# A state-space scan on one Trainium2 core: rows of C moved by 14 columns, seven more products with B on GpSimd, ScalarE's steps reordered in the first and last chunk

## The chip, the core and the metric

The program runs on one core of a Trainium2 chip. A core has five engines that run their own instruction streams and meet at semaphores: TensorE (PE in the profile, PEld for its weight loads), VectorE (DVE), ScalarE (ACT), GpSimd (POOL) and SyncE (SP), whose queue issues the DMAs here. The metric is the device time of the whole program in microseconds; lower is better.

## The reference

Four layers follow each other on an activation of 4 x 1024 x 256 numbers: a Mamba block, a feed-forward block with retrieved experts, a linear attention block, and the feed-forward block again. The change is in the Mamba block alone. After projections, a convolution of four taps and silu, it computes for each token `delta`, `Bm` and `Cm` and then a recurrence along the tokens with 512 channels and 16 states:

```
def step(h, inp):
    d_l, b_l, c_l, x_l = inp
    h = jnp.exp(d_l[:, :, None] * A) * h + (d_l * x_l)[:, :, None] * b_l[:, None, :]
    y_l = jnp.einsum('ben,bn->be', h, c_l)
    return (h, y_l)
```

Then `y + x * W_D`, a product with `silu(skip)`, an output projection, and the residual.

## The kernel before, in words

The tokens are handled in 8 chunks of 512 (`CHUNKS`, c below; an even chunk starts a sequence, an odd chunk continues it). The 512 channels lie as 4 blocks of 128 partitions, and a pass over a chunk takes 2 of them. A *unit* M is one of the 16 states in one pass: 32 units in a chunk, 256 in all; i is a unit's number in its chunk. A unit's work goes round the engines:

- ScalarE computes the decays, exp(delta * A), one per block, into one of three PSUM slots (`decay`, L796).
- (delta * x) times the row of B goes into one of six slots of the buffer U. VectorE does it (L950) from a row that TensorE has spread over the partitions in PSUM (`spread_B`, L524), or GpSimd does it (L363, three units ahead, `AHEAD`) from a row fetched by DMA into the buffer B. Which units are GpSimd's stands in `FIRST_POOL` (first 16 units) and `ON_POOL`.
- VectorE runs the recurrence over the 512 tokens, two scans in a unit (L967), in place in U, one column to the right of a slot's start.
- GpSimd multiplies the scanned state by the row of C (L396), writing it one column to the left, at the slot's start. Rows of C are fetched by DMA into a ring of eight rows of 512 columns, buffer C. The last unit's product is VectorE's.
- TensorE adds up the states with eight transposing matmuls (`nsum`, L543).

Around this, each chunk's projections are computed a chunk ahead, a step in each unit. The tables `PE_AT`, `ACT_AT`, `DVE_AT` and `POOL_AT` say which step an engine does in unit i, after that unit's own work; an engine does all its work in that order, so a step that waits holds up what stands behind it. `"first"` replaces slots in the first chunk, `"late"` adds steps in the last. The steps named below: `in` and `cv` (input projection and convolution of a block, copied out of PSUM by ScalarE: L695, L704), `silu_x` (silu of the convolved chunk, L775) and `silu_g` (silu of the gate, L787), each with a table load ahead and behind, `double` (L650, four instructions on the residual), `sum` and `square` (L731, L738: row statistics of a later chunk), and `gate` (VectorE, L935). In unit M ScalarE first does the two decays of unit M + 1, and only then its steps.

Semaphores bind the rings: decay number s waits until scan s - 3 is done; a product with B for unit M waits until unit M - 6 is summed (`nsum_done`); SyncE's queue issues the fetches in order, each behind the GpSimd product that frees its slot.

The built program puts U at byte 181,216 of a partition, C at 205,856 and B at 222,240.

Of the kernel before, what the change touches and what calls it, by code (L numbers as in the profile page):

```python
# [14 lines left out]
P = 128  # L15
BATCH, SEQ, D = 4, 1024, 256
TOKENS = BATCH * SEQ
CHUNK = 512
CHUNKS = TOKENS // CHUNK
TILES = CHUNK // P  # L20
KD = D // P
E, N, R, TAPS = 512, 16, 128, 4
# [5 lines left out]
def need(eng, sem, value):  # L28

    if isinstance(value, int) and value <= 0:  # L30
        return
    eng.wait_ge(sem, value)
# [28 lines left out]
PASSES = 2  # L61
PE_E = KE // PASSES
UNITS = PASSES * N
ALL_UNITS = CHUNKS * UNITS


def mamba(nc, res, dram, shared, norms):
# [7 lines left out]

    WARM = 4
    U_RING, C_RING, A_RING, B_RING = 6, 8, 3, 2
    FIRST_POOL, AHEAD = (3, 7, 10, 12, 15), 3
    ON_POOL = ((2, 4, 7, 9, 12, 14), (3, 7, 11, 14), (2, 4, 6, 9, 11, 13, 15), (2, 5, 8, 11, 14))
    ctx = ExitStack()  # L80
    with ctx:
        def sb(name, shape, dt=FP32):
            return ctx.enter_context(nc.sbuf_tensor("m_" + name, shape, dt))
# [39 lines left out]
        def blocks(quarter):  # L123
# [7 lines left out]
        stack = sb("stack", [P, 2, CHUNK], FP32R)  # L131
        U = sb("U", [P, U_RING, PE_E, CHUNK + 1])
        state, weighted = U[:, :, :, 1:], U[:, :, :, 0:CHUNK]
        C = sb("C", [P, C_RING, CHUNK])
        B = sb("B", [P, B_RING, CHUNK + 1])[:, :, 1:]
        rows = sb("rows", [2 * N, CHUNK])
        bc_rows = nc.dram_tensor("bc_rows", (2, 2 * N, CHUNK), FP32, kind="Internal").ap()
# [43 lines left out]
                          for d, name in ((0, "turn0"), (0, "turn1"), (2, "query"))] + [(29, "back1", CHUNKS - 1)]}  # L181
# [6 lines left out]
                  "late": [(0, "sum", 8), (1, "square", 8), (2, "sum", 9), (3, "square", 9), (7, "norm", 8),  # L188
                           (8, "sum", 10), (9, "turn0", 8), (9, "turn1", 8), (10, "norm", 9), (11, "query", 8),
                           (12, "turn0", 9), (12, "turn1", 9), (14, "query", 9), (16, "square", 10), (18, "sum", 11),  # L190
                           (19, "square", 11), (20, "norm", 10), (21, "high0", 0), (22, "turn0", 10),
# [61 lines left out]
            c, q, p, n = place(M)  # L253
            return UNITS // 2 * (c // 2) + (N * p + n) // 2 + 1

        pool_units = [M for M in range(ALL_UNITS) if M % N in (ON_POOL[M // N % (2 * PASSES)] if M >= N else FIRST_POOL)]
        BEFORE = [len([m for m in pool_units if m < M]) for M in range(ALL_UNITS)]

        def pair(p):
# [8 lines left out]
        def _(sp):  # L268
# [20 lines left out]
            for M in range(ALL_UNITS):  # L289
# [21 lines left out]
                if FETCH <= M < FETCH + PARTS:  # L311
                    i, at = (M - FETCH) // KE, slice(CHUNK * ((M - FETCH) % KE), CHUNK * ((M - FETCH) % KE + 1))
                    sp.dma_start(shared.even[:, i, at], dram["ffn_w"][:, i, at]).then_inc(w_ffn, 16)
                need(sp, hc_ready, M - C_RING + 1)
                sp.dma_start(C[:, M % C_RING, :],
                             bc_rows[q, N + n:N + n + 1, :].to_broadcast([P, CHUNK])).then_inc(C_ready[M % C_RING], 16)
# [311 lines left out]
        def _(act):  # L628
# [153 lines left out]
            def silu_gate(k):  # L782

                for t in range(TILES):
                    wait_freed(act, f"sk{t}", k)
                g = gate[k % 2][:, :, :]
                nc.scalar.activation(g, g, ACT.Silu).then_inc(gate_ready, 1)  # L787
# [47 lines left out]
            for M in range(ALL_UNITS):  # L835
                if M == 0:
                    part("dl2", 0)
                ahead = M + 2 if M < 2 else M + 1
                if M != 2 and ahead < ALL_UNITS:
                    decay(PE_E * ahead)  # L840
                    decay(PE_E * ahead + 1)
                if M == 0:
                    part("sk3", 0)
                elif M == 1:
                    part("dt3", 0)
                elif M == 3:
                    part("dl3", 0)
                elif M in (5, 8):
                    part("double", M // 8)
                for name, k in parts_of(ACT_AT, M):  # L850
                    if name[:4] == "silu" and (name, k) != ("silu_g", 0):
                        (silu_x if name == "silu_x" else silu_gate)(k)
                        if (name, k) == ("silu_x", 1):
                            silu_gate(0)
                        nc.scalar.preload_act_table_set(EXP_LN_SET)
                    elif name[:4] == "silu":
                        continue
                    else:
                        part(name, k)
            for name in ("high2", "high3"):  # L860
# [1454 lines left out]
```

## Time and profile before

| | us |
|---|---|
| median of 3 runs (lowest, highest) | 1789.19 (1787.57, 1790.89) |
| the profiled execution | 1791.06 |
| its span, first to last instruction | 1789.3 |
| of which the 8 chunks of scans (31.6 to 851.6) | 820.0 |

The span is what the rows below divide up; 1.8 us of the execution lie outside it. Instructions of one engine overlap a little at their ends: for work back to back, the distance between two starts is what an instruction costs, and it is some hundredths of a us less than the duration shown (four in 8.60 us with the next start at 8.57, for one). "Idle before" an instruction names what ended the wait.

### The profile page before, as it was taken

Reading aid. Unit: us, or ns where it says so; the run is one execution under the profiler, and the core shown is the slowest. Engines: PE = TensorE matmul, PEld = TensorE weight load, DVE = VectorE, ACT = ScalarE, POOL = GpSimd, SP = SyncE. Lnnn points to the kernel's source line nnn. Section 1 sums busy time; section 2 is a strip of 40 time slices with the busy share of each in tenths; the row PEclk is TensorE's granted clock in tenths of the full one; section 3 lists DMA queues with packets and bytes.
Section 4 is the critical chain, followed back from the end, with each engine's and each line's share of the span. In section 5 each row is a group of like instructions: output and inputs, shape, how many; then the busy total and the mean of one; then the engine's idle time right before and its main releaser. Section 6 shows DMA issues by size and latency. Waiting matters only on the chain. (4 is left out here: it accounts for less than half of the span.)

```text
span 1789.3 us, 26479 instructions
## 1 busy us (share of the span) xinstructions
PE 1686.4 (94%) x9294; PEld 1330.9 (74%) x9294; DVE 1453.3 (81%) x2301; ACT 1068.6 (60%) x1872; POOL 1063.4 (59%) x668
## 2 busy tenths in 40 slices
PE   8989999899999999877999999999999999999999
PEld 3556666666766666566888888888899788888888
DVE  6899999999999999999877777775366876666665
ACT  7887887878887886878443444433444444344442
POOL 3899999999999998999722222221445322222220
PEclk9999999999999999989999999999999999999999
DMA  6323433343433334362011111121000021111111
GB/s 214 107 94 111 120 112 114 105 127 107 115 106 111 122 109 119 97 214 80 17 38 26 29 33 36 34 54 30 1 0 1 1 60 44 45 43 48 48 47 38
DMA packets 116542, 132.18 MB, mean 74 GB/s; under 512 B 19008, under 2 KB 65216, under 8 KB 116288
## 3 DMA queue, kind: packets, MB, share of 16 engines
q1 hardware_dynamic: 116416, 130.59, 25.4%
q8 instruction: 69, 1.13, 0.2%
q14 instruction: 57, 0.47, 0.1%
HBM read 102.22 MB, written 4.72 MB: 60 GB/s over the span
## 5 line engine op out<-in xcount | busy, mean ns | idle before, releaser
L396 POOL TENSOR_TENSOR m_U<-m_U,m_C 128x1024 f32<-128x1024 f32 x255 | 554.3, 2193 | 43.0 <-DVE m_U L967 43.0
L543 PEld LDWEIGHTS m_y<-ident,m_U 128*128 128x128 f32 x2048 | 248.5, 146 | 106.7 <-issue 72.6
L967 DVE TENSOR_TENSOR_SCAN m_U<-m_dA,m_carry,m_U 128x512 f32<-128x512 f32 x256 | 309.8, 1264 | 9.3 <-ACT m_dA L796 8.5
L967 DVE TENSOR_TENSOR_SCAN m_U<-m_dA,m_U 128x512 f32<-128x512 f32 x256 | 295.2, 1204 | 11.3 <-ACT m_dA L796 11.3
L543 PE MATMUL m_y<-ident,m_U 128*128 128x128 f32 x2048 | 280.0, 282 | 20.0 <-POOL m_U L396 19.5
L796 ACT ACTIVATE m_dA<-high,m_negA 128x512 f32<-128x512 f32 x256 | 170.9, 684 | 57.1 <-DVE m_U L967 56.6
L796 ACT ACTIVATE m_dA<-even,m_negA 128x512 f32<-128x512 f32 x256 | 169.5, 683 | 42.0 <-DVE m_U L967 40.2
L1266 POOL TENSOR_TENSOR SW<-g_Rt 128x512 f32<-128x512 f32 x32 | 39.7, 1271 | 256.8 <-DMA g_CT<-SW 237.1
L1266 POOL TENSOR_TENSOR SW<-f_Rt 128x512 f32<-128x512 f32 x32 | 41.0, 1309 | 213.4 <-DMA f_CT<-SW 213.4
L524 PE MATMUL m_psB<-m_stack,m_pick 128*128 128x512 f32 x169 | 86.1, 509 | 40.0 <-DVE m_U L950 38.1
L1455 ACT ACTIVATE g_sil<-g_psG 128x512 f32<-128x512 f32 x64 | 38.3, 599 | 126.9 <-PE g_psG L1325 126.9
L1455 ACT ACTIVATE f_sil<-f_psG 128x512 f32<-128x512 f32 x64 | 38.3, 598 | 126.3 <-PE f_psG L1325 126.2
L1368 PE MATMUL f_psO<-weights_hi,f_H_hi 128*128 128x256 f32 x384 | 108.9, 284 | 4.8 <-DVE f_H_lo L1622 4.7
L1368 PE MATMUL g_psO<-weights_hi,g_H_hi 128*128 128x256 f32 x384 | 108.4, 282 | 0.7 <-DVE g_H_lo L1622 0.6
L1368 PE MATMUL f_psO<-weights_hi,f_H_lo 128*128 128x256 f32 x384 | 107.5, 280 | 0.0
L1368 PE MATMUL f_psO<-weights_lo,f_H_hi 128*128 128x256 f32 x384 | 107.5, 280 | 0.0
L1368 PE MATMUL g_psO<-weights_hi,g_H_lo 128*128 128x256 f32 x384 | 107.2, 279 | 0.0
L1368 PE MATMUL g_psO<-weights_lo,g_H_hi 128*128 128x256 f32 x384 | 107.2, 279 | 0.0
L433 PE MATMUL m_job<-turned 128*128 128x512 f32 x224 | 106.1, 596 | 0.7 <-ACT even L713 0.5
L950 DVE TENSOR_TENSOR m_U<-even,m_psB 128x1024 f32<-128x1024 f32 x88 | 105.1, 1195 | 0.6 <-PE m_psB L524 0.6
L1618 DVE TENSOR_TENSOR zns<-g_psU,g_sil 128x512 f32<-128x512 f32 x64 | 44.0, 688 | 73.9 <-PE g_psU L1325 72.5
L1842 POOL TENSOR_TENSOR a_rinv<-a_ssq,a_mhalf 128x64 f32<-128x64 f32 x6 | 63.2, 10549 | 59.0 <-DVE a_ssq L2117 59.0
(412 smaller groups left out, 4459.3 us busy)
## 6 DMA issues: line engine op xcount, KB each, us to landing
m_C<-bc_rows SPq DMA_DIRECT2D x256, 256.0 KB, 3.2
m_B<-bc_rows SPq DMA_DIRECT2D x87, 256.0 KB, 3.5
f_CT<-SW SPq DMA_DIRECT2D x128, 64.0 KB, 2.1
g_CT<-SW SPq DMA_DIRECT2D x128, 64.0 KB, 2.1
even<-in_ffn_w SPq DMA_DIRECT2D x16, 256.0 KB, 5.4
g_z_raw<-g_turned_z SPq DMA_DIRECT2D x112, 32.0 KB, 1.9
out<-res SPq DMA_DIRECT2D x7, 512.0 KB, 2.8
res<-in_x SPq DMA_DIRECT2D x1, 3072.0 KB, 12.6
```

The source lines that it names most:

```text
L396: pool.tensor_tensor(weighted[:, at, :, :], state[:, at, :, :], C[:, M % C_RING, :].unsqueeze(1).to_broadcast([P, PE_E, CHUNK]), ALU.mult) ...
L433: ins = nc.tensor.matmul(out, w, x, start=first and k == 0, stop=last and k == len(pairs) - 1)
L524: nc.tensor.matmul(psB[:, :], pick[:, n:n + 1].to_broadcast([P, P]), stack[:, q, :], start=True, stop=True).then_inc(B_full, 1)
L543: last = nc.tensor.matmul(y[:, t, j * P:(j + 1) * P], weighted[:, M % U_RING, j, t * P:(t + 1) * P], ident[:, :], start=False, stop=n == N ...
L796: nc.scalar.activation(dA[:, s % A_RING, :], delta[q][:, e, :], ACT.Exp, scale=negA[:, e, n:n + 1]).then_inc(dA_ready, 1)
L950: nc.vector.tensor_tensor(state[:, M % U_RING, :, :], dx[q][:, pair(p), :], psB[:, :].unsqueeze(1).to_broadcast([P, PE_E, CHUNK]), ALU.mul ...
L967: nc.vector.tensor_tensor_scan(u, dA[:, s % A_RING, :], u, carry[:, e, n:n + 1] if q else 0.0, ALU.mult, ALU.add).then_inc(scan_done, 1)
L1266: pool.tensor_tensor(S[:, j, :, :], Rt[:, j // 2, 0, j % 2, 0:TOP].unsqueeze(2).to_broadcast(SPREAD), Rt[:, j // 2, 1, j % 2, :].unsqueeze ...
L1368: last = nc.tensor.matmul(psO[:, j // 2, (j % 2) * D:(j % 2 + 1) * D], H[a][:, i % RING, j * P:(j + 1) * P], lower[b][:, i, :], start=i == ...
L1455: nc.scalar.activation(to[:, i % 2, :], psG[:, i % 2, :], ACT.Silu).then_inc(g_free, 1)
L1618: nc.vector.tensor_tensor(to, u, s, ALU.mult).then_inc(u_free, 1)
L1842: pool.tensor_tensor(rinv[:, at, :], ssq[:, at, :], mhalf[:, :, :], ALU.pow).then_inc(rinv_ready, 1)
```

## The change

C's buffer gets 14 more columns, and its rows begin 14 columns (56 bytes) further; U stays, B and what lies behind it moves by 64 bytes (B to 222,304). GpSimd's units are now given for all 16 passes: 9 in chunk 0 as before (three of them others), 13 instead of 12 in chunks 1, 3, 5 and 7, 11 instead of 10 in chunks 2, 4 and 6; 94 in all instead of 87. In the first chunk ScalarE does `double` in units 6 and 17 and no longer in 5 and 8, `cv0` and `in1` in unit 5 and no longer in 4, and the gate's silu for chunk 0 in unit 15, by itself, and no longer right behind `silu_x` in unit 13. In the last chunk `sum` and `square` for piece 9 move from units 2 and 3 to units 3 and 6.

```diff
-    FIRST_POOL, AHEAD = (3, 7, 10, 12, 15), 3
-    ON_POOL = ((2, 4, 7, 9, 12, 14), (3, 7, 11, 14), (2, 4, 6, 9, 11, 13, 15), (2, 5, 8, 11, 14))
+    EVEN, ODD, AHEAD = ((1, 3, 5, 7, 9, 11, 13), (3, 7, 11, 14)), ((1, 3, 5, 7, 9, 11, 13), (2, 4, 7, 9, 12, 14)), 3
+    ON_POOL = ((3, 7, 9, 11, 13), (3, 7, 11, 14)) + (ODD + EVEN) * (CHUNKS // 2 - 1) + ((1, 4, 7, 9, 12, 14), (2, 4, 6, 8, 10, 12, 14))
...
-        C = sb("C", [P, C_RING, CHUNK])
+        C = sb("C", [P, C_RING * CHUNK + 14])[:, 14:].rearrange("p (r t) -> p r t", r=C_RING)
...
-                  "first": {3: (), 4: ("cv0", "in1")},
-                  "late": [(0, "sum", 8), (1, "square", 8), (2, "sum", 9), (3, "square", 9), (7, "norm", 8),
+                  "first": {2: (), 3: (), 4: (), 5: ("cv0", "in1"), 15: ("silu_g",)},
+                  "late": [(0, "sum", 8), (1, "square", 8), (3, "sum", 9), (6, "square", 9), (7, "norm", 8),
...
-                elif M in (5, 8):
-                    part("double", M // 8)
+                elif M in (6, 17):
+                    part("double", M // 17)
                 for name, k in parts_of(ACT_AT, M):
-                    if name[:4] == "silu" and (name, k) != ("silu_g", 0):
+                    if name[:4] == "silu":
                         (silu_x if name == "silu_x" else silu_gate)(k)
-                        if (name, k) == ("silu_x", 1):
-                            silu_gate(0)
                         nc.scalar.preload_act_table_set(EXP_LN_SET)
-                    elif name[:4] == "silu":
-                        continue
```

On ScalarE, in the first chunk around units 3 to 9 (m_dA: decays, high: `cv`, turned: `in`, res: `double`, m_rn: `sum`):

```order
 L796 ACTIVATE m_dA<-even,m_negA 128x512 x2
 L713 ACTIVATE even<-m_job 128x512
-L796 ACTIVATE m_dA<-even,m_negA 128x512 x2
+L796 ACTIVATE m_dA<-even,m_negA 128x512 x4
 L704 ACTIVATE high<-m_job,m_convb 128x512
 L695 ACTIVATE turned<-m_job 128x512
 L796 ACTIVATE m_dA<-even,m_negA 128x512 x2
 L650 ACTIVATE res<-res,m_sc 128x256 x4
-L796 ACTIVATE m_dA<-even,m_negA 128x512 x2
-L704 ACTIVATE high<-m_job,m_convb 128x512
-L796 ACTIVATE m_dA<-even,m_negA 128x512 x2
-L695 ACTIVATE turned<-m_job 128x512
```

Two more decays stand ahead of the first convolution's copy. On the same engine in units 13 to 17 (L775: `silu_x`, L787: `silu_g`), now:

```order
81 L775 ACT_TABLE_LOAD
82 L775 ACTIVATE high<-high 128x2048
83 L853 ACT_TABLE_LOAD
84 L796 ACTIVATE m_dA<-even,m_negA 128x512 x4
85 L787 ACT_TABLE_LOAD
86 L787 ACTIVATE even<-even 128x2048
87 L853 ACT_TABLE_LOAD
```

Before, L787 stood directly behind L775 with one table load on each side of the pair; now four decays stand between the two, and there are two table loads more. On VectorE in the middle of chunk 1 (the rows with m_psB are its products with B), before:

```order
95 L967 SCALAR_TENSOR_TENSOR m_U<-m_dA,m_carry,m_U 128x512 x4
96 L950 TENSOR_TENSOR m_U<-high,m_psB 128x2x512
97 L967 SCALAR_TENSOR_TENSOR m_U<-m_dA,m_carry,m_U 128x512 x4
98 L950 TENSOR_TENSOR m_U<-high,m_psB 128x2x512
99 L967 SCALAR_TENSOR_TENSOR m_U<-m_dA,m_carry,m_U 128x512 x2
```

and now, where the same instructions have the lines 963 and 946:

```order
94 L963 SCALAR_TENSOR_TENSOR m_U<-m_dA,m_carry,m_U 128x512 x4
95 L946 TENSOR_TENSOR m_U<-high,m_psB 128x2x512
96 L963 SCALAR_TENSOR_TENSOR m_U<-m_dA,m_carry,m_U 128x512 x2
97 L946 TENSOR_TENSOR m_U<-high,m_psB 128x2x512
98 L963 SCALAR_TENSOR_TENSOR m_U<-m_dA,m_carry,m_U 128x512 x2
99 L946 TENSOR_TENSOR m_U<-high,m_psB 128x2x512
100 L963 SCALAR_TENSOR_TENSOR m_U<-m_dA,m_carry,m_U 128x512 x2
```

Both pieces run from the scans of units 11 and 12 to those of unit 15. Between them VectorE made two products (for units 14 and 16) and makes three now (14, 15 and 16); the product for unit 1 has gone to GpSimd instead, and of units 2 to 13 VectorE makes six before and now.

## Rows read from the trace of the kernel before

**Rows 1.** The page, part 1: busy time, share and instructions by engine.
```profile
PE 1686.4 (94%) x9294; PEld 1330.9 (74%) x9294; DVE 1453.3 (81%) x2301; ACT 1068.6 (60%) x1872; POOL 1063.4 (59%) x668
```

**Rows 2.** Windows by chunk (0, 1, 2, 7, rest): length, busy time by engine, clock, DMA.
```profile
31.60:143.30 111.70, 95.42 (x426) 58.46 (x424) 102.21 (x93) 90.59 (x159) 95.72 (x66) 0.96 0.34 112
...
143.30:245.50 102.20, 96.24 (x471) 65.53 (x469) 100.36 (x87) 82.25 (x140) 100.30 (x56) 0.97 0.39 115
245.50:345.20 99.70, 93.70 (x471) 63.62 (x471) 98.66 (x89) 82.07 (x140) 96.97 (x66) 0.99 0.37 111
...
749.20:851.60 102.40, 74.17 (x418) 60.46 (x418) 98.36 (x85) 83.69 (x174) 99.48 (x63) 0.87 0.43 137
851.60:1789.30 937.70, 919.58 (x5570) 812.07 (x5570) 637.21 (x1558) 386.50 (x686) 269.56 (x162) 1.00 0.14 32
```

**Rows 3.** Waits in chunks 1 to 6: total us, times, longest.
```profile
DVE m_U L967 <- ACT m_dA L796: 8.5, 12, 1.4
...
POOL m_U L396 <- DVE m_U L967: 14.7, 19, 1.2
...
PE m_psB L524 <- DVE m_U L950: 16.3, 26, 1.4
```

**Rows 4.** Groups of instructions by form, up to 860 us: busy us, mean ns.
```profile
L396 POOL TENSOR_TENSOR m_U<-m_U,m_C 128x1024 f32<-128x1024 f32 x255 | 554.3, 2193 | 43.0 <-DVE m_U L967 43.0
...
L363 POOL TENSOR_TENSOR m_U<-high,m_B 128x1024 f32<-128x1024 f32 x48 | 96.4, 2008 | 0.0
...
L352 POOL TENSOR_TENSOR high<-high 128x512 f32<-128x512 f32 x16 | 20.7, 1291 | 0.0
...
L381 POOL TENSOR_TENSOR turned<-ident,m_convw 128x512 f32<-128x512 f32 x4 | 4.0, 1038 | 0.0
...
L345 POOL TENSOR_TENSOR m_sc<-m_sc,m_off 128x8 f32<-128x8 f32 x7 | 1.4, 203 | 0.1
```

**Rows 5.** Timeline of GpSimd around the end of chunk 1: start, length, instruction.
```profile
238.95 8.60 POOL L396 TENSOR_TENSOR m_U<-m_U,m_C 128x1024 f32<-128x1024 f32 x4
247.52 1.99 POOL L363 TENSOR_TENSOR m_U<-even,m_B 128x1024 f32<-128x1024 f32 x1
249.47 4.32 POOL L396 TENSOR_TENSOR m_U<-m_U,m_C 128x1024 f32<-128x1024 f32 x2
```

**Rows 6.** Timeline of VectorE in chunks 1 and 2, units 13 to 16.
```profile
183.47 4.79 DVE L967 TENSOR_TENSOR_SCAN m_U<-m_dA,m_carry,m_U 128x512 f32<-128x512 f32 x4
188.19 1.19 DVE L950 TENSOR_TENSOR m_U<-high,m_psB 128x1024 f32<-128x1024 f32 x1
190.80 2.46 DVE L967 TENSOR_TENSOR_SCAN m_U<-m_dA,m_carry,m_U 128x512 f32<-128x512 f32 x2 [1.42 <-ACT m_dA L796]
...
291.48 2.34 DVE L967 TENSOR_TENSOR_SCAN m_U<-m_dA,m_U 128x512 f32<-128x512 f32 x2 [0.57 <-ACT m_dA L796]
```

**Rows 7.** Timeline of VectorE in chunk 0: the scans behind a wait.
```profile
57.16 2.34 DVE L967 TENSOR_TENSOR_SCAN m_U<-m_dA,m_U 128x512 f32<-128x512 f32 x2 [3.52 <-ACT m_dA L796]
...
70.42 4.57 DVE L967 TENSOR_TENSOR_SCAN m_U<-m_dA,m_U 128x512 f32<-128x512 f32 x4 [0.86 <-ACT m_dA L796]
...
88.44 2.34 DVE L967 TENSOR_TENSOR_SCAN m_U<-m_dA,m_U 128x512 f32<-128x512 f32 x2 [3.40 <-ACT m_dA L796]
```

**Rows 8.** Timeline of ScalarE in chunk 0.
```profile
54.16 0.69 ACT L704 ACTIVATE high<-m_job,m_convb 128x512 f32<-128x512 f32 x1 [3.54 <-PE m_job L433]
...
57.60 2.06 ACT L650 ACTIVATE res<-res,m_sc 128x256 f32<-128x256 f32 x4
...
61.29 0.69 ACT L704 ACTIVATE high<-m_job,m_convb 128x512 f32<-128x512 f32 x1 [0.44 <-PE m_job L433]
...
84.44 1.89 ACT L787 ACTIVATE even<-even 128x2048 f32<-128x2048 f32 x1
86.35 1.28 ACT L855 ACT_TABLE_LOAD   x1
```

**Rows 9.** Timeline of VectorE in chunk 7, units 4 and 5.
```profile
764.59 2.46 DVE L967 TENSOR_TENSOR_SCAN m_U<-m_dA,m_carry,m_U 128x512 f32<-128x512 f32 x2 [2.54 <-ACT m_dA L796]
767.78 2.46 DVE L967 TENSOR_TENSOR_SCAN m_U<-m_dA,m_carry,m_U 128x512 f32<-128x512 f32 x2 [0.73 <-ACT m_dA L796]
```

**Rows 10.** The page, part 6: DMA issues, KB each, us to landing.
```profile
m_C<-bc_rows SPq DMA_DIRECT2D x256, 256.0 KB, 3.2
m_B<-bc_rows SPq DMA_DIRECT2D x87, 256.0 KB, 3.5
```

More of the change, by code:

```diff
@@ L254, in copied @@
             return UNITS // 2 * (c // 2) + (N * p + n) // 2 + 1
-        pool_units = [M for M in range(ALL_UNITS) if M % N in (ON_POOL[M // N % (2 * PASSES)] if M >= N else FIRST_POOL)]
+        pool_units = [M for M in range(ALL_UNITS) if M % N in ON_POOL[M // N]]
         BEFORE = [len([m for m in pool_units if m < M]) for M in range(ALL_UNITS)]
```

## The prediction

> **What bounds the kernel now.** I read the windows by chunk first. Of 1789.3 us, 937.7 lie behind the scans, where nothing changes [rows 2]; the change lives in the 820 us of the eight chunks. There three engines are nearly full, which the page's shares over the whole span hide [rows 1]. In chunk 1 VectorE works 100.4 us of 102.2, GpSimd 100.3 and TensorE 96.2; in chunk 2 it is 98.7, 97.0 and 93.7 of 99.7 [rows 2]. The waits come second: in the six middle chunks VectorE waits 8.5 us in all, always for a decay from ScalarE, GpSimd 14.7 us for scans, and TensorE 16.3 us for VectorE's products [rows 3]. VectorE is thus the engine that sets the pace; GpSimd is as full in the odd chunks and has 1.7 us more room in the even ones; and every long wait of VectorE's is ScalarE's doing. The timelines come last and place those waits: in chunk 0 before units 6, 10 and 15, 3.52 + 0.86 + 3.40 us [rows 7], in chunk 7 before units 4 and 5, 2.54 + 0.73 us [rows 9], and in the middle chunks 1.42 us before unit 15 of an odd and 0.57 us of an even one [rows 6].
>
> **The seven products.** One more unit in each of chunks 1 to 7 goes from VectorE to GpSimd. VectorE loses 7 products: 1.19 us each, less the 0.07 by which neighbours overlap (four scans of 4.79 us in all have the next start at 4.72), so 1.11 us, 7.8 us in all [rows 6]. GpSimd gains 7 at 249.47 - 247.52 = 1.95 us [rows 5], 13.7 us more, in the scans' shadow only if it has room. It has 102.2 - 100.3 = 1.9 us in an odd chunk and 2.7 in an even one [rows 2]. So without anything else GpSimd would be full in the odd chunks. TensorE spreads seven rows fewer, which nobody waits for.
>
> **The rows of C.** This decides whether that room exists. No row shows a product with C at the new place, so I bound it. GpSimd's two-input products differ in time for the same size: 512 columns take 1.291 us where both inputs and the output start at the same place modulo 2048 bytes (`dx`, L352), and 1.038 us for L381, whose inputs start over 1,000 bytes apart modulo 2048 but also repeat elements [rows 4]. With the 0.203 us of an eight-column product taken as fixed, 1024 columns would take 2 x 1.291 - 0.2 = 2.38 us in the one case and 2 x 1.038 - 0.2 = 1.88 us in the other. Between these lie the two measured at 1024: 2.193 for C and 2.008 for B [rows 4]. From the buffers' places, C's rows start 16 to 60 bytes beyond the state that they multiply (modulo 2048), B's rows 932 bytes or more from their other input. 14 columns make C's distance 72 to 116 bytes. I take B's 2.01 us, the nearest product of the same size whose inputs are not close, and keep 1.88 and 2.38 as ends. 32 products a chunk at 0.185 us less free 5.9 us: GpSimd then needs 100.3 + 1.95 - 5.9 = 96.4 us in an odd and 93.0 in an even chunk, below VectorE's 98 to 99. The gain over the present time is then VectorE's alone, since faster products with C take nothing off its path. GpSimd stops being the bound once 32 products save 2.1 us, at 2.13 us for one.
>
> The Trainium skill speaks against this: GPSIMD Engine Reference, Performance versus the Vector engine, gives about 2.6 cycles an element to any two-input product, from its two inputs sharing a read port, and knows no influence of where they lie. As an estimate from that page, 1024 elements would take 2.2 us before and after. C's 2.19 us agrees; B's 2.01 does not, nor does L352's 1.29 us where the rule gives 1.1. By the rule the sum would be that of the first rival below.
>
> The fetch of C's rows to the new place I cost at nothing: rows of B, which already start off by 4 bytes, land in 3.5 us against 3.2 [rows 10], and a ring of eight rows fetches 7 units, over 20 us, ahead.
>
> **Where the freed VectorE time goes: middle chunks.** In an odd chunk VectorE now has three products ahead of units 14, 15 and 16 instead of two, while ScalarE does `silu_x`. That covers 1.1 of the 1.42 us of wait before unit 15; I take 0.9, as in the even chunks a wait of 0.57 is left with this very pattern [rows 6]. Odd: 1.1 + 0.9 = 2.0 us, three chunks 6.0. Even: the product alone and 0.1 us of wait, 1.2, three chunks 3.6.
>
> **Chunk 0.** The wait of 3.52 us before unit 6 stands because ScalarE sits 3.54 us in the copy of `cv0` until TensorE has done the convolution [rows 7, 8], with the decays for unit 6 queued behind. Now the decays for units 5 and 6 go first, so unit 6 starts on time. But TensorE is late with the next piece as well: `cv1` arrives at 61.3 us whatever ScalarE does [rows 8], and the decays for unit 8 stand behind it, so they end at about 62.5. VectorE comes to unit 8 at about 59.4 and waits 3 us there, where the scan of unit 8 began at 63.9 before. Only 1.4 us are gained by then, of which 1.1 are a product with B that unit 9 gives to GpSimd earlier than unit 10 did. `double` out of unit 8 (2.0 us) removes the 0.86 before unit 10, and `silu_g` out of unit 13 (1.89 us) with one product more on VectorE takes the 3.40 down to some 0.4; the block moved to unit 15, 4.5 us with its own two table loads, costs 0.3 to 0.6 again, like its kind in even chunks. VectorE's share of products in the chunk is the same. Followed unit by unit, unit 17 then starts about 4 us earlier, and `double` in unit 17 and the gate at unit 18 stand in slots with room. I take 4.0; the ends are 1.5 (TensorE holds the pace of units 3 to 12) and 6.5.
>
> **Chunk 7.** `sum` out of unit 2 leaves only `silu_g` there: 1.8 to 2.0 us of the 2.54 go. The 0.73 before unit 5 goes too, since the product for unit 6 is VectorE's now. GpSimd's next use of these statistics is in unit 7, after the product with C, and `square` in unit 6 ends before. With the product moved: 2.7 + 1.1, of which I take 3.5, as ScalarE has `square` and `norm` next to each other now.
>
> **Sum.** 4.0 + 6.0 + 3.6 + 3.5 = 17.1 us. The lead of the decays before units 5 to 12 is only 1 to 2 us, and TensorE has 5 % left; I give back 1.6 for waits that this brings. So 1791.06 - 15.5 = 1775.6 for an execution like the profiled one; the median lies 1.9 us lower, hence 1773.7.
>
> **Rivals.**
> First, *the product with C keeps its 2.19 us*, since its price comes from writing one column beside its own input. For: the six slots of U put C 16 to 60 bytes away, and the products agree within 0.01 us, so distance may count for nothing. Then GpSimd is full in chunks 1 to 6: +0.5 us in odd ones, 0 in even ones; chunk 0 keeps its 4 us, chunk 7 gives 2: 1789.2 - 4.5 = 1784.7.
> Second, *ScalarE and TensorE take the gain*: C becomes cheaper, but the waits for decays come back elsewhere at half of what was removed. For: VectorE already meets decays with no lead at units 4 and 15; against: three of the four moves take work off ScalarE where it is late. 1789.2 - 8 = 1781.
> Third, and slower: *the new place is worse*, up to the 2.38 us bound. Place: L396 in all chunks; price 256 times the difference, since GpSimd is then the bound. From the first rival's 4.5 us of gain, the kernel turns slower by over 3.6 us from 8.1 / 256 = 0.03 us on, at 2.225 us; at 2.38 it is +48 - 4.5, 1833. Against it: 72 bytes is farther from the coincident case than 16.
> That the products don't move, or that the steps wait for something behind them, I exclude from the order of the instructions.
>
> **How the numbers follow.** What measurement tells from no change is 0.2 %, 3.6 us. Forecast 0.60 (1768 to 1780); first rival 0.20 (1781 to 1789, two thirds of it faster by over 3.6 us); second 0.10, faster; third 0.10, slower. Faster 0.60 + 0.10 + 0.13 = 0.83, same 0.07, slower 0.10. The range goes from 1766, where nearly all of VectorE's waits are gone in chunk 0, to 1788: it takes in the forecast and both mild rivals.
>
> **What the profile after would show.** L396 at 2.01 us or, by the rivals, at 2.19 or over 2.22: this one row decides most. L363 near 2.01, 94 of them, VectorE's products 161 in place of 168. Waits of VectorE in chunks 1 to 6 below 7 us, all for decays; 1.42 before unit 15 of an odd chunk down to about 0.5; GpSimd's waits for scans up from 14.7 to over 35 us. Chunk 0 at about 107.7, odd chunks 100.2, even ones 98.5, chunk 7 at 98.9. In chunk 0 the wait before unit 6 moves to unit 8. I am wrong if GpSimd waits less than now, if chunk 0 keeps its length, or if anything behind 852 us changes its length by over 1 us.

## The result and the profile after

| | before | after |
|---|---|---|
| median, us (lowest, highest, 10 runs each, same chip) | 1790.77 (1787.57, 1792.31) | 1795.76 (1793.62, 1796.91) |
| span of the profiled execution | 1789.3 | 1794.5 |

The ratio is 1.003, with a 95% interval of 1.0021 to 1.0039: the change makes the kernel 0.3% slower. The forecast was 1773.7, in a range that ended at 1788, with a chance of 0.10 for slower.

The row that was to decide most is that of the product with C. Groups of instructions by form in the profile after (busy us, mean ns of one, then the idle time ahead of them), to be set beside [rows 4]:

```profile
L396 POOL TENSOR_TENSOR m_U<-m_U,m_C 128x1024 f32<-128x1024 f32 x255 | 554.7, 2191 | 34.6 <-DVE m_U L963 34.6
L963 DVE TENSOR_TENSOR_SCAN m_U<-m_dA,m_carry,m_U 128x512 f32<-128x512 f32 x256 | 310.4, 1269 | 13.4 <-POOL m_U L363 8.7 <-ACT m_dA L796 4.0
L963 DVE TENSOR_TENSOR_SCAN m_U<-m_dA,m_U 128x512 f32<-128x512 f32 x256 | 295.9, 1207 | 15.0 <-POOL m_U L363 8.4 <-ACT m_dA L796 6.4
L363 POOL TENSOR_TENSOR m_U<-high,m_B 128x1024 f32<-128x1024 f32 x52 | 104.5, 2010 | 1.2 <-issue 1.2
L363 POOL TENSOR_TENSOR m_U<-even,m_B 128x1024 f32<-128x1024 f32 x42 | 84.2, 2004 | 0.5 <-PE m_y L543 0.5
L352 POOL TENSOR_TENSOR high<-high 128x512 f32<-128x512 f32 x16 | 20.5, 1282 | 0.0
```

It is 2191 ns, against 2193 before: the new place did nothing. GpSimd has the seven more products with B (94 in all) and no time saved for them. VectorE's scans waited almost only for decays before (0.6 us for L363):

```profile
L967 DVE TENSOR_TENSOR_SCAN m_U<-m_dA,m_carry,m_U 128x512 f32<-128x512 f32 x256 | 309.8, 1264 | 9.3 <-ACT m_dA L796 8.5 <-POOL m_U L363 0.6
L967 DVE TENSOR_TENSOR_SCAN m_U<-m_dA,m_U 128x512 f32<-128x512 f32 x256 | 295.2, 1204 | 11.3 <-ACT m_dA L796 11.3
```

Now they wait 17.1 us for L363 (8.7 + 8.4). Windows by chunk (0, 1, 2, 7, rest: length, then busy time by engine, clock, DMA), to be set beside [rows 2]:

```profile
32.10:138.60 106.50, 92.25 (x421) 56.65 (x420) 101.22 (x92) 92.10 (x160) 94.62 (x66) 0.98 0.36 116
138.60:241.70 103.10, 96.11 (x469) 63.65 (x468) 99.82 (x87) 82.59 (x140) 101.44 (x56) 0.98 0.38 116
241.70:343.50 101.80, 95.09 (x474) 63.88 (x473) 98.06 (x88) 82.39 (x141) 99.62 (x68) 0.99 0.40 112
753.00:856.60 103.60, 76.17 (x411) 63.48 (x410) 98.64 (x85) 84.53 (x175) 101.03 (x64) 0.81 0.45 139
856.60:1794.50 937.90, 921.08 (x5584) 813.29 (x5583) 638.59 (x1558) 386.69 (x686) 271.65 (x163) 1.00 0.14 32
```

Chunk 0 is 5.2 us shorter, chunks 1 to 6 are 8.5 us longer together (0.8 to 1.1 in an odd one, 1.6 to 2.1 in an even one), chunk 7 is 1.2 longer. The windows are cut at a chunk's first scan, and VectorE's product for a chunk's unit 1 stands just ahead of that scan (before: 1.19 us at 142.15, the scan at 143.26). Unit 1 is GpSimd's now in chunks 1 to 7, which takes this product out of the window of the chunk before: about 1.1 of chunk 0's 5.2 us belong to the table of chunk 1, as the run with that table alone shows below. What follows the scans has its length. VectorE's busy time in chunk 2 fell by 0.6 us while the chunk grew by 2.1, and GpSimd is busy for 99.6 of 101.8 and 101.4 of 103.1. The waits in chunks 1 to 6 (total us, times, longest), to be set beside [rows 3]:

```profile
DVE m_U L963 <- POOL m_U L363: 14.6, 24, 1.6
POOL m_U L396 <- DVE m_U L963: 12.3, 12, 1.3
PE m_psB L524 <- DVE m_U L946: 11.9, 29, 0.8
DVE m_U L963 <- ACT m_dA L796: 4.6, 12, 0.5
```

VectorE's waits for decays fell from 8.5 to 4.6, as forecast (below 7), but 14.6 us for GpSimd came in their place. GpSimd's own waits for scans fell from 14.7 to 12.3 us, which the prediction had named as a sign of being wrong. Where VectorE's waits stand is seen in the timelines of chunk 2, first pass (start, length, instruction, in brackets the idle time before it). GpSimd, then VectorE:

```profile
262.29 2.00 POOL L363 TENSOR_TENSOR m_U<-even,m_B 128x1024 f32<-128x1024 f32 x1
264.25 2.19 POOL L396 TENSOR_TENSOR m_U<-m_U,m_C 128x1024 f32<-128x1024 f32 x1
266.38 0.19 POOL L400 COPY m_carry<-m_U 128x4 f32<-128x4 f32 x1
266.52 2.18 POOL L396 TENSOR_TENSOR m_U<-m_U,m_C 128x1024 f32<-128x1024 f32 x1
268.66 2.00 POOL L363 TENSOR_TENSOR m_U<-even,m_B 128x1024 f32<-128x1024 f32 x1
```
```profile
264.32 4.57 DVE L963 TENSOR_TENSOR_SCAN m_U<-m_dA,m_U 128x512 f32<-128x512 f32 x4 [0.45 <-POOL m_U L363]
268.81 1.20 DVE L946 TENSOR_TENSOR m_U<-even,m_psB 128x1024 f32<-128x1024 f32 x1
270.69 4.57 DVE L963 TENSOR_TENSOR_SCAN m_U<-m_dA,m_U 128x512 f32<-128x512 f32 x4 [0.69 <-POOL m_U L363]
```

With a product with B every other unit, GpSimd needs 268.66 - 262.29 = 6.37 us for two units and VectorE, without its wait, 270.69 - 264.32 - 0.69 = 5.68. GpSimd loses its lead, and then each pair of units costs 0.69 us more. The waits come back at every other unit up to 13, 2.8 us in an even chunk. In an odd chunk they are 1.9 to 2.7 us, and most of it, 1.56 us, stands at unit 30, in the second pass.

In chunk 0 the wait of 3.52 us before unit 6 is gone; waits of 1.12 us before the product between the scans of units 6 and 7 and of 2.21 us before unit 8 stand in its place, and 3.40 us before unit 15 [rows 7] are 0.65:

```profile
57.40 1.22 DVE L946 TENSOR_TENSOR m_U<-even,m_psB 128x1024 f32<-128x1024 f32 x1 [1.12 <-PE m_psB L524]
63.09 2.34 DVE L963 TENSOR_TENSOR_SCAN m_U<-m_dA,m_U 128x512 f32<-128x512 f32 x2 [2.21 <-ACT m_dA L796]
85.28 2.34 DVE L963 TENSOR_TENSOR_SCAN m_U<-m_dA,m_U 128x512 f32<-128x512 f32 x2 [0.65 <-ACT m_dA L796]
```

The wait of 1.42 us before unit 15 of an odd chunk [rows 6] is down as well, here in chunk 1:

```profile
187.08 2.46 DVE L963 TENSOR_TENSOR_SCAN m_U<-m_dA,m_carry,m_U 128x512 f32<-128x512 f32 x2 [0.30 <-ACT m_dA L796]
```

In chunk 7, 2.54 and 0.73 us [rows 9] are 0.29 and nothing, and others appear further on:

```profile
767.48 2.46 DVE L963 TENSOR_TENSOR_SCAN m_U<-m_dA,m_carry,m_U 128x512 f32<-128x512 f32 x2 [0.29 <-ACT m_dA L796]
783.55 2.46 DVE L963 TENSOR_TENSOR_SCAN m_U<-m_dA,m_carry,m_U 128x512 f32<-128x512 f32 x2 [0.84 <-POOL m_U L363]
793.79 4.81 DVE L963 TENSOR_TENSOR_SCAN m_U<-m_dA,m_carry,m_U 128x512 f32<-128x512 f32 x4 [0.84 <-POOL m_U L363]
835.79 2.46 DVE L963 TENSOR_TENSOR_SCAN m_U<-m_dA,m_carry,m_U 128x512 f32<-128x512 f32 x2 [1.88 <-ACT m_dA L796]
```

### The profile page after: what moved, and what is told of

The parts are those of the page before. It is cut to its first block and busy times, and to the rows that moved or that the text cites. A ratio compares the mean times of both kernels' runs of the same rounds, so it can differ in the third digit from the quotient of the medians.

```text
span 1794.5 us, 26477 instructions
## 1 busy us (share of the span) xinstructions
PE 1691.0 (94%) x9287; PEld 1331.0 (74%) x9287; DVE 1450.0 (81%) x2294; ACT 1073.0 (60%) x1874; POOL 1076.9 (60%) x675
## 5 line engine op out<-in xcount | busy, mean ns | idle before, releaser
L396 POOL TENSOR_TENSOR m_U<-m_U,m_C 128x1024 f32<-128x1024 f32 x255 | 554.7, 2191 | 34.6 <-DVE m_U L963 34.6
L543 PE MATMUL m_y<-ident,m_U 128*128 128x128 f32 x2048 | 284.3, 285 | 35.6 <-POOL m_U L396 34.9
L363 POOL TENSOR_TENSOR m_U<-high,m_B 128x1024 f32<-128x1024 f32 x52 | 104.5, 2010 | 1.2 <-issue 1.2
L946 DVE TENSOR_TENSOR m_U<-even,m_psB 128x1024 f32<-128x1024 f32 x85 | 101.8, 1198 | 1.7 <-PE m_psB L524 1.7
```

The lines of the kernel that those rows point to most:

```text
L363: pool.tensor_tensor(state[:, M % U_RING, :, :], dx[q][:, pair(p), :], B[:, i % B_RING, :].unsqueeze(1).to_broadcast([P, PE_E, CHUNK]), AL ...
L396: pool.tensor_tensor(weighted[:, at, :, :], state[:, at, :, :], C[:, M % C_RING, :].unsqueeze(1).to_broadcast([P, PE_E, CHUNK]), ALU.mult) ...
L543: last = nc.tensor.matmul(y[:, t, j * P:(j + 1) * P], weighted[:, M % U_RING, j, t * P:(t + 1) * P], ident[:, :], start=False, stop=n == N ...
L946: nc.vector.tensor_tensor(state[:, M % U_RING, :, :], dx[q][:, pair(p), :], psB[:, :].unsqueeze(1).to_broadcast([P, PE_E, CHUNK]), ALU.mul ...
```

## Experiments: the change taken apart

Two questions stood after the traces: is the loss all in the middle chunks' table, and why is the product with C where it was? The next four kernels are each a part of the change, put on the kernel before.

**Only the rows of C moved.**

```diff
-        C = sb("C", [P, C_RING, CHUNK])
+        C = sb("C", [P, C_RING * CHUNK + 14])[:, 14:].rearrange("p (r t) -> p r t", r=C_RING)
```

> The kernel before with C's rows 14 columns further and nothing else. My theory: the place of C does nothing, the product with C (L396) stays at 2.19 us and the time within 2 us of before. The forecast's theory, which the trace after already speaks against: L396 at 2.01 us. A third: the move costs (B and the buffers behind C shift by 64 bytes, the rows' DMAs land unaligned), then L363 or the fetches get slower and the time rises by 2 us or more.

Measured: 1.0007 (0.9998 to 1.0016), no difference. Its row:

```profile
L396 POOL TENSOR_TENSOR m_U<-m_U,m_C 128x1024 f32<-128x1024 f32 x255 | 553.6, 2190 | 43.1 <-DVE m_U L967 43.1
```

The place of C alone changes neither price nor time, and the fetches land in 3.3 us against 3.2 [rows 10]. In the changed kernel they take 3.7 us, but so they do in the next run, where C is at its old place: that comes with the table and not with the address, and no wait of GpSimd's for them appears.

**Only the table of chunks 1 to 6.**

```diff
-    ON_POOL = ((2, 4, 7, 9, 12, 14), (3, 7, 11, 14), (2, 4, 6, 9, 11, 13, 15), (2, 5, 8, 11, 14))
+    EVEN, ODD = ((1, 3, 5, 7, 9, 11, 13), (3, 7, 11, 14)), ((1, 3, 5, 7, 9, 11, 13), (2, 4, 7, 9, 12, 14))
```

> The kernel before with the new list of GpSimd's units in chunks 1 to 6 alone (13 and 11 products a chunk). My theory: in passes with units 1, 3, ..., 13 on GpSimd two products with C and one with B take 6.2 us for each two units against VectorE's 5.6 to 5.8, VectorE waits for GpSimd's products, and chunks 1 to 6 get 8 to 9 us longer in all; the time is 7 to 10 us above before. The first rival's pricing: GpSimd is just full, chunks 1 to 6 change by +1.5 us at most. If the loss in the changed kernel came from ScalarE's or C's part, this one is near before or faster.

Measured: 1.0049 (1.0035 to 1.0062), 8 to 9 us slower, with VectorE's waits in chunks 1 to 6:

```profile
DVE m_U L967 <- POOL m_U L363: 14.8, 26, 1.6
DVE m_U L967 <- ACT m_dA L796: 5.2, 13, 0.7
```

The 14.8 us are those of the changed kernel (14.6). The loss is this table's, at a product of 2.19 us. Chunk 0, in which this run changes nothing, is 110.5 us against 111.7: the product for unit 1 of chunk 1 has left its end, and VectorE is busy there for 101.07 us against 102.21 [rows 2].

```profile
31.40:141.90 110.50, 94.19 (x421) 57.44 (x420) 101.07 (x92) 89.90 (x158) 94.64 (x66) 0.96 0.36 112
```

**Only ScalarE's order.** The ScalarE lines of the diff ("first", "late", `double`, `silu_g`), nothing else.

> The kernel before with ScalarE's new order in chunks 0 and 7 alone, all products where they were. My theory: chunk 0 is 3.5 to 5 us shorter (the wait before unit 6 gone, one of about 2.2 us at unit 8 in its place), chunk 7 1.5 to 2.5 us shorter, chunks 1 to 6 as before: 5 to 7.5 us faster. Rival: the gains belong to the products that moved with it (unit 9 in place of 10 in chunk 0, unit 6's in chunk 7) and ScalarE's order alone brings less than 3 us.

Measured: 0.9978 (0.9969 to 0.9987), 4 us faster, 1 us short of the low end expected. Chunk 0 is 108.0 us (111.7 before), chunk 7 100.8 (102.4), 3.7 and 1.6 us less and both at the low end of what was expected. The profiled executions differ by 6.1 us and the medians by 3.7; where the rest goes isn't shown, but what lies behind the chunks took 935.0 to 939.1 us in the profiles here, though no kernel changes it. The wait expected at unit 8 isn't there: VectorE waits 1.11 and 1.95 us for rows from TensorE, before two of its products.

**ScalarE's order and the new lists of chunks 0 and 7.**

```diff
+    FIRST, LAST = ((3, 7, 9, 11, 13), (3, 7, 11, 14)), ((1, 4, 7, 9, 12, 14), (2, 4, 6, 8, 10, 12, 14))
```

> ScalarE's new order and the new lists for chunks 0 and 7, but the old lists in chunks 1 to 6 and C at its old place. My theory: chunk 0 is 4 to 5 us shorter, chunk 7 0 to 1 us longer as in the changed kernel (13 products in it make GpSimd late at units 9, 12 and 25), so 3 to 5 us faster than before and 1 to 3 us slower than the kernel with ScalarE's order alone. Rival: chunk 7's loss in the changed kernel is inherited from the full GpSimd of chunks 1 to 6; then this one is the faster of the two, by 2 to 4 us.

Measured: 0.998 (0.9971 to 0.9989), as far below before as ScalarE's order alone; the 1 to 3 us between the two that were expected didn't show. Chunk 0 is 107.6 us, 4.1 shorter, and chunk 7 102.7: its 13 products give back the 1.6 us that ScalarE's order brings there, with a wait of 0.84 us for L363 at unit 12 and one of 1.85 for a decay at unit 25, though chunks 1 to 6 are the old ones. So most of that loss is chunk 7's own and not inherited; the wait at unit 9 isn't there and came with the middle chunks' table. Chunk 6 is 99.0 us against 99.7, since the product for unit 1 of chunk 7 has left its end, so that the 13th product costs about 1 us over both chunks. The three parts' ratios add to 1.0007 + 1.0049 + 0.998 - 2 = 1.0036, where the whole has 1.003: within the intervals nothing is left for an interplay.

## Experiments: what the product with C costs, and why

**Prices.** A kernel that leaves the order of work alone and varies what the product reads and writes; the four forms stand at lines 398, 400, 402 and 404. In odd chunks the second to fourth leave sums other than the reference's.

```diff
-        C = sb("C", [P, C_RING, CHUNK])
+        C = sb("C", [P, C_RING, CHUNK + 65])[:, :, 0:CHUNK]
...
-    U_RING, C_RING, A_RING, B_RING = 6, 8, 3, 2
+    U_RING, C_RING, A_RING, B_RING = 6, 7, 3, 2
...
+                    if q == 0 or M % 4 == 0 or M >= SECOND_LAST:
+                        pool.tensor_tensor(weighted[:, at, :, :], state[:, at, :, :], row, ALU.mult)
+                    elif M % 4 == 1:
+                        pool.tensor_tensor(state[:, at, :, :], state[:, at, :, :], row, ALU.mult)
+                    elif M % 4 == 2:
+                        pool.tensor_tensor(weighted[:, at, :, :], dx[q][:, pair(p), :], row, ALU.mult)
+                    else:
+                        pool.tensor_tensor(weighted[:, at, :, :], weighted[:, at, :, :], row, ALU.mult)
```

> The price of the product with C by itself, in the kernel before. C's ring has seven rows, each 260 bytes (an odd number of columns) further from the next modulo 2048 bytes, so that a row of C starts 20 to 1,060 bytes from the state it multiplies. In odd chunks the product has four forms by unit: as before (state to one column left), in place at the state's column, from dx instead of the state to the slot's start, and in place at the slot's start; the third and fourth leave y wrong in odd chunks. My theory: distance does nothing (2.19 us at all seven rows) and the 0.18 us above the product with B come from reading what is written one column beside: the third form, which has the operands of a product with B, takes 2.01 us, the in-place ones 2.19 or 2.01. The forecast's theory: far rows take 2.01 us or less, near ones 2.19. A third: the port is shared with TensorE or VectorE, and all forms take what falls beside them, spread over 1.9 to 2.3 us.

Measured once: 1791.85 us (before 1791.62). The groups of this run look like the kernel before:

```profile
L398 POOL TENSOR_TENSOR m_U<-m_U,m_C 128x1024 f32<-128x1024 f32 x183 | 398.9, 2192 | 38.6 <-DVE m_U L973 38.3
L404 POOL TENSOR_TENSOR m_U<-m_U,m_C 128x1024 f32<-128x1024 f32 x24 | 52.4, 2183 | 3.3 <-DVE m_U L973 3.3
L400 POOL TENSOR_TENSOR m_U<-m_U,m_C 128x1024 f32<-128x1024 f32 x24 | 51.7, 2156 | 0.9 <-DVE m_U L973 0.8
L402 POOL TENSOR_TENSOR m_U<-high,m_C 128x1024 f32<-128x1024 f32 x24 | 51.7, 2154 | 0.2
```

But these means hide three prices. The timeline of GpSimd in chunk 2 has neighbours that differ by 0.2 us at one line:

```profile
260.61 2.42 POOL L398 TENSOR_TENSOR m_U<-m_U,m_C 128x1024 f32<-128x1024 f32 x1 [1.43 <-DVE m_U L973]
...
267.19 2.22 POOL L398 TENSOR_TENSOR m_U<-m_U,m_C 128x1024 f32<-128x1024 f32 x1
...
271.29 2.04 POOL L398 TENSOR_TENSOR m_U<-m_U,m_C 128x1024 f32<-128x1024 f32 x1
```

None of the theories holds as written. A far row is not faster than a near one, the operands' kind does nothing, and what falls beside a product does nothing. The distance in hundreds of bytes sorts nothing either: slot 0 of U, with the rows of C, gives 2.20, 2.40, 2.18, 2.00, 2.18, 2.38, 2.18 us in turn. Sorted by the address of the first input less that of the second, modulo 16 bytes, for each of the two blocks of 512 elements, all 255 products fall into place (worked out from each one's length and the buffers' addresses):

```
first less second input, modulo 16: block 1, block 2     units   mean us of the forms
0, 4  (also 0, 0 and 4, 4)                                 61     2.36 to 2.38
4, 8                                                       66     2.18 to 2.19
12, 0                                                      62     2.18 to 2.19
8, 12 (also 8, 8 and 12, 12)                               66     2.00
```

So half a product, 512 elements with half of what is fixed, costs 1.19 us where the difference is 0 or 4 and 1.00 where it is 8 or 12. The lengths in the four classes don't overlap: 2.34 to 2.42, twice 2.17 to 2.24, and 1.99 to 2.04 us. Neither address alone does it: at L398, with the first block of the state 4 beyond a multiple of 16, rows of C at 0, 4, 8 and 12 give 2.19, 2.38, 2.19 and 2.00 us, and with it at 12 they give 2.18, 2.01, 2.19 and 2.37. Where the output goes makes no difference (L398 and L400 agree class by class within 0.01 us). This also explains the rows of before: a slot of U is 4,104 bytes, 8 modulo 16, and a block in it 2,052, 4 modulo 16. The state is therefore 4 and 8 beyond C in even slots and 12 and 0 in odd ones: one half slow and one fast in each. A shift by 14 columns is 8 modulo 16 and exchanges the two cases. With such slots any shift of C averages 2.19 us. B lies 12 or 8 off in all 87 products: 2.01. And `dx` (L352) has difference 0: 1.28 us.

Two pages of the Trainium skill bear on this. SBUF — State Buffer, Specifications (TRN2), gives the memory lines of 16 bytes, and a penalty for each crossing into a new line; it says nothing of two inputs' offset. The period found here is the same 16 bytes; that the lines cause it isn't shown. GPSIMD Engine Reference, 3. Performance versus the Vector engine, gives any two-input product about 2.6 cycles an element at 1.2 GHz: as an estimate 2.2 us for 1024, about what the slow case has without the 0.2 us that is fixed (2.38 - 0.20 = 2.18); the fast case, 1.80, lies below what the page calls the floor.

**What the schedule would do at 2.02 us.** The changed kernel with the product over 936 of 1024 elements.

```diff
-                    pool.tensor_tensor(weighted[:, at, :, :], state[:, at, :, :],
+                    pool.tensor_tensor(weighted[:, at, :, 0:468], state[:, at, :, 0:468],
```

> The changed kernel with its product with C over 468 of 512 columns (936 elements in place of 1024), which leaves 44 columns of each unit unmultiplied: by (2.19 - 0.20) / 1024 for an element it should take 2.02 us, what the forecast took for the product at the new place. If the product's price is the step that failed and the rest of the forecast holds, the time is 1774 (1768 to 1780) and VectorE waits for GpSimd's products under 3 us. If the forecast's other terms were wrong too, chunks 1 to 6 stay over 100 us each and the time is 1782 or more.

Measured: 1776.23, 0.9919 (0.9906 to 0.9933). The price came out at 2.03 us, scans waited 2.0 us for L363 in all, and chunks 1 to 6 lasted 99.1 to 101.0 us. With the price, the time is within the forecast's 1768 to 1780; chunk 7, at 100.4 us where 98.9 was forecast, isn't put right by it.

**Slots of 4,112 bytes, C three columns further.** On the kernel before, then on the changed one (the padded kernel below).

```diff
-        U = sb("U", [P, U_RING, PE_E, CHUNK + 1])
+        U = sb("U", [P, U_RING, PE_E * (CHUNK + 1) + 2])[:, :, 0:PE_E * (CHUNK + 1)].rearrange("p u (e t) -> p u e t", e=PE_E)
...
+        C = sb("C", [P, C_RING * CHUNK + 3])[:, 3:].rearrange("p (r t) -> p r t", r=C_RING)
```

> The kernel before with two columns of padding in each slot of U (so that a slot is 4,112 bytes, a multiple of 16, instead of 4,104) and C's rows 3 columns further; nothing else. From the 255 products with C in the run on prices: a half of a product (512 elements) takes 1.19 us where the address of the first input less that of the second is 0 or 4 modulo 16 bytes, and 1.00 where it is 8 or 12. Here the state lies 8 bytes (first block) and 12 bytes (second) beyond C modulo 16 in every slot, so L396 takes 2.00 us in all 255, without a row at 2.19. Rival: the padding or some other place decides, and L396 stays at 2.19 or splits. Time: GpSimd gets 6 us more room a chunk, but VectorE's path is as it was, so 0 to 4 us faster than before.

> The changed kernel with the same padding of U and C's rows 3 columns further in place of 14. Theory: the product takes 2.00 us in all slots, VectorE's waits for GpSimd's products go from 17 us to under 3, and the time is within 3 us of the run with the product cut to 936 columns: 1773 to 1779. Rival: that run gained from the columns left out (TensorE or the memory less busy), and with all columns at 2.00 us the time stays above 1782.

On the kernel before: 0.9999 (0.999 to 1.0008). On the changed kernel: 1774.05 us, 0.9906 (0.9891 to 0.9921), 17 us faster than the kernel before beside it (1791.07) and the fastest of all kernels here. The rows, of the first and the second:

```profile
L396 POOL TENSOR_TENSOR m_U<-m_U,m_C 128x1024 f32<-128x1024 f32 x255 | 508.8, 2008 | 86.2 <-DVE m_U L967 85.6
```
```profile
L396 POOL TENSOR_TENSOR m_U<-m_U,m_C 128x1024 f32<-128x1024 f32 x255 | 510.9, 2018 | 56.8 <-DVE m_U L963 54.5 <-PE m_y L543 1.8
L963 DVE TENSOR_TENSOR_SCAN m_U<-m_dA,m_carry,m_U 128x512 f32<-128x512 f32 x256 | 309.7, 1262 | 3.9 <-ACT m_dA L796 2.7 <-POOL m_U L363 1.3
```

The price fell to 2.01 and 2.02 us, with no product above 2.08. With the old table the 45 us saved turned into waiting (43.0 to 86.2 us) and bought nothing; with the new table they carry the seven products. Windows of the second kernel's chunks 0, 1, 2 and 7:

```profile
31.90:138.70 106.80, 94.62 (x428) 58.78 (x427) 101.29 (x92) 92.16 (x160) 91.18 (x67) 0.95 0.36 116
138.70:238.40 99.70, 93.32 (x464) 62.32 (x463) 99.14 (x86) 82.45 (x140) 94.58 (x55) 0.99 0.43 120
238.40:337.30 98.90, 95.17 (x485) 65.54 (x484) 97.62 (x88) 82.11 (x140) 95.20 (x69) 0.99 0.37 116
...
735.40:836.40 101.00, 72.66 (x413) 58.65 (x412) 98.41 (x85) 84.43 (x175) 94.29 (x63) 0.86 0.45 141
```

**C one column further instead of three**, on the kernel before with the same slots: both blocks slow.

> The kernel before with the padding of U and C's rows 1 column further: first block 0, second block 4 bytes modulo 16 beyond C, in every slot. Two columns, 8 bytes, from the kernel with 3. Theory: L396 takes 2.37 us in all 255 units, GpSimd is the bound, and the time is 255 x 0.19 = 47 us above before, less the 15 us that GpSimd waits for scans in the middle chunks and some 10 in the outer ones: 1815 to 1835. Rival: with rows this near the state, nothing but the padding counts, and the price is as with 3 columns.

Measured once: 1817.19 us, 26 above before.

```profile
L396 POOL TENSOR_TENSOR m_U<-m_U,m_C 128x1024 f32<-128x1024 f32 x255 | 601.3, 2385 | 23.2 <-DVE m_U L967 23.2
```

Two columns of a buffer's place, with the same schedule, are 0.38 us a product and 27 us in all. The products took 47 us more of GpSimd (601.3 against 554.3), of which 20 came out of its waiting for scans (43.0 to 23.2).

## Experiments: how full GpSimd may be

**Ten products a chunk, but dense**, on the kernel before.

```diff
+    EVEN = ((1, 3, 5, 7, 9, 11, 13), (3, 7, 11))
```

> The kernel before with the even chunks' first pass on the new list (units 1, 3, ..., 13) and their second on 3, 7 and 11: ten products a chunk, as many as before. My theory: where GpSimd's products stand counts, not their sum; with one every other unit GpSimd falls behind by 0.3 to 0.6 us for each two units in the first pass, VectorE waits there for 1.5 to 3 us, and in the second pass VectorE has one product more and cannot catch up: 1.5 to 2.5 us a chunk, 5 to 8 us in all. The rival, that GpSimd's load over the whole chunk sets the time: within 1 us a chunk of before, 0 to 2 us in all.

Measured: 1.0035 (1.0022 to 1.0049). Even chunks last 103.2 us against 99.7, odd ones 0.5 to 1.4 less than before, as the product for an even chunk's unit 1 has left their end; both together are 2.6 longer. VectorE waited 6.2 us for L363 in chunks 1 to 6, and made one product more in the second pass, where GpSimd had time over. The same number of products in worse places costs 6 to 7 us. Chunk 2:

```profile
243.90:347.10 103.20, 94.01 (x472) 62.91 (x469) 100.12 (x90) 82.82 (x141) 99.55 (x68) 0.99 0.35 111
```

**Eleven, spread**, with ScalarE's new order and the new list of chunk 0.

```diff
+    EVEN = ((2, 4, 7, 9, 12, 14), (2, 5, 8, 11, 14))
```

> ScalarE's new order, the new list for chunk 0, the old ones for odd chunks and 7, and in even chunks eleven products, spread as 2, 4, 7, 9, 12, 14 and 2, 5, 8, 11, 14. As many products as the changed kernel has in even chunks, without its dense pass. My theory: even chunks get up to 1.1 us shorter than the 99.7 of before, since both passes have room on GpSimd: 1781 to 1785, up to 3 us faster than with the old lists. The rival by total load: GpSimd full at 99 us, even chunks as before or up to 1 us longer: 1786 to 1788.

Measured: 1784.81 us, 0.9965 (0.9952 to 0.9979). The time alone lies in the range of my theory, but ScalarE's order alone had 0.9978, and the intervals overlap, so it doesn't decide. The lengths do: even chunks took 99.6 to 100.8 us, no less than with ten, and GpSimd is busy for 98.5 of 100.3 in chunk 2. By them my theory of a gain was wrong and the rival by total load right.

```profile
240.70:341.00 100.30, 94.19 (x468) 63.97 (x469) 97.86 (x89) 82.07 (x140) 98.54 (x67) 0.99 0.37 112
```

Both counts matter: at 2.19 us eleven products fill GpSimd's even chunk, and set densely, as in the changed kernel, they cost another 1.5 us a chunk.

**One product more in each of chunks 1 to 6, at 2.01 us.**

```diff
+    EVEN, ODD = ((1, 3, 5, 7, 9, 11, 13), (2, 5, 8, 11, 14)), ((1, 3, 5, 7, 9, 11, 13), (2, 4, 6, 8, 10, 12, 14))
```

> The kernel of the run before this one with one more product with B on GpSimd in each of chunks 1 to 6: 14 in odd ones, 12 in even ones. GpSimd has about 5 us of room in an odd and 3.5 in an even chunk and needs 2.0 more; VectorE loses 1.1 us a chunk. If VectorE sets the pace there, up to 6 us faster than the run before; if TensorE (94 us of 99) or GpSimd's delays in a dense pass take over, no gain or 1 to 4 us slower.

Measured: 1777.19, 0.9928 (0.9915 to 0.9942), 3 us slower than the padded kernel. Even chunks are 0.4 us shorter (98.5), odd ones 1 to 2 us longer (101.5): scans wait 6.1 us for L363 again, most of it in the odd chunks' second dense pass. Twelve in even chunks with 13 in odd ones wasn't tried; as an estimate from these lengths it would bring about 1 us.

## Why the prediction was wrong, step by step

- **The rows of C: wrong, and the step that failed.** The prediction took B's 2.01 us for the new place, on a distance modulo 2048 bytes. It measured 2191 ns. With it went the 5.9 us of room a chunk that the sum rested on: the middle chunks, forecast 9.6 us shorter, are 8.5 longer. What counts is the offset modulo 16 bytes, and 56 bytes only exchange the two kinds of slots. The bounds, from L352 and from L381, held: the worst case was put at 2.38 us and measured 2.385; the best, 1.88, was reached nowhere, the fast kind takes 2.00. But between the bounds the value was chosen by likeness in size, where the rows already held a hint against it, which the first rival names: a product whose mean is within 0.01 us of 2.19 in all six slots shows no trace of a distance that varies from 16 to 60 bytes, and nothing showed why one of 72 to 116 should act.
- **The seven products: right.** GpSimd's busy time in chunks 1 and 2 rose by 1.1 and 2.7 us. VectorE makes 161 products in 193.0 us where it made 168 in 200.6. Its whole busy time fell by 3.3 us only (1453.3 [rows 1] to 1450.0): its scans take 1.3 us more in all and the work behind the chunks 1.4, and 1.6 us stay unplaced. In the padded kernel, where it waits little, it is busy for 1.2 us less in chunk 1 and 1.0 less in chunk 2, which is the 1.1 us a product of the forecast.
- **The fetches at nothing: right**, 3.3 us against 3.2 in the run with C alone, and nobody waits for the 3.7 of the changed kernel.
- **Middle chunks: right on its condition.** With the product at 2.02 us (padded slots) the odd chunks are 6.3 us shorter in all against 6.0 forecast, the even ones 2.8 against 3.6. The wait before unit 15 of an odd chunk fell from 1.42 [rows 6] to 0.30 us even in the changed kernel. GpSimd's waits for scans were forecast at over 35 us and are 28.1; the forecast's own lengths gave no more, 3 x (100.2 - 96.4) + 3 x (98.5 - 93.0) = 27.9.
- **Chunk 0: right, 4.0.** In the run with the ends alone it is 107.6 against 111.7. The wait moved to unit 8 as said (2.21 us, 3 forecast), with 1.12 before a product that was not foreseen. The 4.9 us in the padded kernel have the 1.1 of the product for unit 1 of chunk 1 in them.
- **Chunk 7: wrong, 3.5 forecast.** ScalarE's order is worth 1.6 us there, and the 13th product takes as much out of that chunk. The working looked at units 2 to 7 alone; the list moved products up to unit 28, and waits appeared at units 9, 12 and 25. Even in padded slots chunk 7 gains 1.4; another 1.1 stand in chunk 6, for the product for unit 1, so about 1 us was forecast too much.
- **The sum.** At the price it assumed, the forecast of 1773.7 met 1774.05 us, in part by luck. The eight chunks are 15.4 us shorter in the padded kernel's profile, against 15.5 forecast; but there chunk 7 was 2.1 us too high, and chunk 0 (4.9) and the 1.6 us of give-back that did not come made up for it. Another 2.1 us lie behind the chunks (935.6 against 937.7), where nothing was changed or forecast, and the kernel before ran at 1791.07 us beside this run and not at 1789.2.
- **First rival: its condition came true, its reason and its time (1784.7) did not.** Writing one column beside the input isn't what costs: the in-place form at the state's column has the same prices. It priced a full GpSimd at +0.5 and 0 us a chunk, from the room in whole chunks. Measured are about +1.0 and +2.0. In an even chunk the list sets seven products in one pass, where GpSimd needs 6.37 us for two units against 5.68, and leaves it room in the other; in an odd one most of the wait stands late in the second pass.
- **Second rival: did not come.** In the padded kernel, where its condition holds, VectorE's waits for decays in chunks 1 to 6 are 4.2 us against 8.5.
- **Third rival: right in its price, wrong in the place.** 2.38 us exists, but 14 columns don't lead to it. It valued the loss at 256 times the difference; with the old table nearly half of that was absorbed.

## What to carry to other kernels

Before a schedule is tuned around an instruction's price, find out what sets that price, from the lengths of single instructions sorted by where their operands lie: a mean over a group (2192 ns) can be three prices. When buffers are rings, look at slot stride and shift together, since a shift can only exchange the slots' cases. And count an engine's room pass by pass, with the pattern of its work, not over a whole chunk; cheaper work off the path (45 us here) was worth nothing with the old table, and with the new one it turned 5 us of loss into 17 us of gain, of which ScalarE's order makes about 4.

## What the runs showed of the hardware that was not expected

In these kernels each half of a GpSimd product of two float32 inputs in unit steps, 512 of 1024 elements, costs 1.00 or 1.19 us by the difference of the inputs' addresses modulo 16 bytes (8 and 12 fast, 0 and 4 slow, first less second), wherever the output lay: 2.01, 2.19 or 2.385 us for 1024. All of 255 products in one run fit, as did 255 at each of two places chosen by it. How VectorE was busy meanwhile made next to no difference: in the kernel before, products with C beside none of VectorE's two-input products took 2192 ns in the mean and those beside a whole one 2200. Products that repeat single elements were not sorted this way, and why 4 differs from 12 stays open.
